# Moments and normalisations of three batches in tile pieces behind the maxima of the cross attention units

## What is computed

```
def _layernorm(x, axis=-1, eps=1e-05):
    m = jnp.mean(x, axis=axis, keepdims=True)
    v = jnp.var(x, axis=axis, keepdims=True)
    return (x - m) / jnp.sqrt(v + eps)

    x = x + _L0_attn_ref(_layernorm(x, axis=-1), ...)
    x = x + _L0_xattn_ref(_layernorm(x, axis=-1), ctx_1024, ctx_1024, ...)
    x = x + _L0_ffn_ref(_layernorm(x, axis=-1), ...)
```

## Time and profile before

| | us |
|---|---|
| median of 3 runs | 828.49 |
| lowest and highest | 826.69, 833.39 |
| the profiled execution | 834.13 |
| its span in the trace | 832.0 |

### The profile page before, as it was taken

How to read it: one execution, slowest core, us unless ns; L and a number is a source line. 1 busy time by engine, 2 the same in 40 slices (tenths; PEclk the granted TensorE clock), 3 DMA queues, 4 the chain that set the end, 5 groups by cost and what they waited for, 6 DMA issues and landing times.

```text
span 832.0 us, 14945 instructions
## 1 busy us (share of the span) xinstructions
PE 676.5 (81%) x4693; PEld 328.5 (39%) x4698; DVE 589.4 (71%) x1606; ACT 414.0 (50%) x708; POOL 282.6 (34%) x502
## 2 busy tenths in 40 slices
PE   2758998989888896079999952677999989998987
PEld 1324454435344444045666631222332323324443
DVE  3857788776556765657878745788889898953574
ACT  1332665655655542013333312156788777885454
POOL 4742454544523144703223220122323142331310
PEclk9875999989988858579999985569999999999898
DMA  7543654482233215211111123321223011000000
GB/s 218 159 175 119 208 181 142 137 274 72 70 99 87 74 42 156 77 33 40 44 41 40 45 68 126 101 77 52 65 90 127 27 52 51 3 2 1 2 25 26
DMA packets 74780, 71.27 MB, mean 86 GB/s; under 512 B 14560, under 2 KB 67168, under 8 KB 74704
## 3 DMA queue, kind: packets, MB, share of 16 engines
q1 hardware_dynamic: 72000, 64.84, 25.3%
q0 software_dynamic: 2272, 4.69, 1.8%
q10 hardware_dynamic: 432, 0.79, 0.3%
HBM read 41.90 MB, written 28.00 MB: 84 GB/s over the span
## 4 chain that ended last, share of the span: by engine, by line
PE 60%; DVE 19%; issue 7%; DMA 5%; POOL 4%; ACT 4%; SPq 1%; DVEq 0%; POOLq 0%; ACTq 0%
PE bank_pv L733 11%; DVE mx L591 11%; PE bank_turn L575 8%; PE bank_scores L2025 5%; PE bank_scores L685 4%; PE bank_scores L1775 4%; PE bank_turn L1760 4%; PE bank_scores L1760 4%; PE bank_turn L752 3%; POOL routed_tokens L1727 2%; PE bank_scores L1768 2%; PE bank_turn L528 2%; DVE stats L450 1%; DMA stk<-stack_A 1%; PE bank_turn L794 1%
## 5 line engine op out<-in xcount | busy, mean ns | idle before, releaser
L591 DVE TENSOR_REDUCE mx<-bank_turn 128x1 f32<-128x512 f32 (+3 forms) x452 | 260.4, 615 | 58.8 <-PE bank_turn L580 29.6
L575 PE MATMUL bank_turn<-stk 64*128 64x128 bf16 (+3 forms) x708 | 164.2, 322 | 31.2 <-DVE mx L591 20.4
L685 PE MATMUL bank_scores<-stk 64*128 64x512 bf16 (+4 forms) x576 | 176.3, 373 | 4.7 <-ACT probs L706 3.6
L710 ACT ACTIVATE probs<-bank_scores 128x1024 f32<-128x1024 f32 (+4 forms) x160 | 116.9, 769 | 101.6 <-PE bank_scores L685 100.3
L706 ACT ACTIVATE probs<-bank_scores 128x512 f32<-128x512 f32 x256 | 138.6, 605 | 35.5 <-PE bank_scores L685 34.5
L733 PE MATMUL bank_pv<-probs,vsl 128*32 128x512 f32 (+4 forms) x1152 | 142.9, 570 | 2.6 <-POOL probs L718 1.6
L575 PEld LDWEIGHTS bank_turn<-stk 64*128 64x128 bf16 x708 | 58.2, 101 | 133.4 <-DVE mx L591 63.9
L718 POOL TENSOR_SCALAR_AFFINE_SELECT probs<-probs 128x256 f32<-128x256 f32 x128 | 51.6, 408 | 72.3 <-ACT probs L710 70.7
L1743 POOL DMA_INDIRECT expert_outputs<-probs,y_at x39 | 37.3, 958 | 101.4 <-DVE probs L1662 98.8
L477 POOL TENSOR_TENSOR rstd<-var,mhalf 128x4 f32<-128x4 f32 x24 | 25.4, 1056 | 115.8 <-DVE var L456 115.7
L1807 ACT COPY okT<-bank_scores 128x512 f32<-128x512 f32 x39 | 22.9, 587 | 81.2 <-PE bank_scores L1768 81.2
(11 more groups left out here) (297 smaller groups left out, 1140.9 us busy)
## 6 DMA issues: line engine op xcount, KB each, us to landing
stk<-stack_A SPq DMA_DIRECT2D x64, 256.0 KB, 3.3
w<-in_M_w SPq DMA_DIRECT2D x12, 512.0 KB, 4.9
stack_A<-parts SPq DMA_DIRECT2D x15, 384.0 KB, 3.1
stack_A<-fill SPq DMA_DIRECT2D x8, 512.0 KB, 5.3
stk<-stack_X SPq DMA_DIRECT2D x16, 256.0 KB, 2.7
stack_A<-parts SPq DMA_DIRECT2D x15, 256.0 KB, 3.3
probs<-routed_tokens SPq DMA_DIRECT2D x39, 65.0 KB, 1.9
b_gated<-in_M_b SPq DMA_DIRECT2D x1, 2048.0 KB, 11.2
```

Of the source, the lines that this page charges most:

```text
L575: mm = e.matmul(o, stk[r, slot, 0, pp, qt * P:(qt + 1) * P], stk[r, slot, 1, pp, 0:keys], start=True, stop=not a.causal)
L591: e.tensor_reduce(o.rearrange("p h q -> p q h"), bank_of((g, m))[:, 0:k * wide].rearrange("p (q h k) -> p q h k", q=len(tiles), h=len(hs)) ...
L685: mm = e.matmul(score_bank(g, kt, i)[0:a.kp, 0:S - q0], stk[r, slot, 1, pp, kt * P:kt * P + a.kp], stk[r, slot, 0, pp, q0:S], start=True, ...
L710: e.activation(probs[0:a.kp, probs_of(g, kt), j:HG:2, 0:n], bank_scores[0:a.kp, 2 * j:2 * j + 2, 0:n], ACT.Exp, scale=1 / math.sqrt(HD)).t ...
```

## The change

A table APART_IN names three units and batches: 20 (X0, 3), 24 (M0, 0), 28 (M0, 1). In such a unit each of the four maxima on VectorE is followed by the `bn_stats` of one tile; the `bn_aggr` and the variance follow `neg`. In the unit after it (21, 25, 29) each of the four maxima is followed by the subtract and multiply of one tile. The blocks of moments in units 19, 23 and 27 and of normalisations in units 20, 24 and 28 are gone. The helpers are split by tile; where they are called for a whole batch they issue what they issued before. NORM_IN is unchanged, so Pool's norm_pool stays in units 20, 24 and 28; the orders of TensorE, ScalarE, Pool and SP are unchanged.

```
-MOMENTS_IN = {5: (X0, 0), 9: (X0, 1), 13: (X0, 2), 19: (X0, 3), 23: (M0, 0), 27: (M0, 1), 31: (M0, 2), 33: (A1, 3), 37: (X1, 0), 40: (F1, 0), 41: (X1, 1),
+MOMENTS_IN = {5: (X0, 0), 9: (X0, 1), 13: (X0, 2), 31: (M0, 2), 33: (A1, 3), 37: (X1, 0), 40: (F1, 0), 41: (X1, 1),
+APART_IN = {20: (X0, 3), 24: (M0, 0), 28: (M0, 1)}
...
         def moments_dve(e, ln, b):
+            for j in range(QT):
+                tile_stats_dve(e, ln, b, j)
+            variance_dve(e, ln, b)
+
+        def tile_stats_dve(e, ln, b, j):
             n = norm_number(ln, b)
+            if j == 0:
+...
+            e.bn_stats(stats[:, j, :], tile_of(4 * b + j)).then_inc(s_stat, 1)
+
+        def variance_dve(e, ln, b):
             e.wait_ge(s_stat, QT * (n + 1))
 ...
+        def normalise_tile(e, ln, b, j):
+            if j == 0:
+...
+            i = e.tensor_scalar(normal(ln, b)[:, j, :], tile_of(4 * b + j), mv[:, j, 0:1], rstd[:, j:j + 1],
+                                ALU.subtract, ALU.mult)
+            if j == QT - 1:
+                i.then_inc(s_xn, 1)
...
                 for i in range(4):
                     for k in beside[i]:
                         max_dve(e, *k)
+                    if g in APART_IN:
+                        after, b = APART_IN[g]
+                        tile_stats_dve(e, after.ln, b, i)
+                    if g - 1 in APART_IN:
+                        after, b = APART_IN[g - 1]
+                        normalise_tile(e, after.ln, b, i)
...
             if a is X0:
                 if g + 2 <= last_of_stream(g):
                     neg_of(e, g + 2)
+                if g in APART_IN:
+                    after, b = APART_IN[g]
+                    variance_dve(e, after.ln, b)
                 beside_dve(e, g - 1, "b")
                 beside_dve(e, g, "a")
-                if g in NORM_IN:
-                    after, b = NORM_IN[g]
-                    normalise(e, after.ln, b)
                 if g in MOMENTS_IN:
```

More of the change, by code:

```diff
@@ L440, in moments_dve @@
         def moments_dve(e, ln, b):
+            for j in range(QT):
+                tile_stats_dve(e, ln, b, j)
+            variance_dve(e, ln, b)
+        def tile_stats_dve(e, ln, b, j):
             n = norm_number(ln, b)
[L443 to L450, removed]
+            if j == 0:
+                if ln == 0:
+                    e.wait_ge(s_x0 if b == 0 else s_x, 16)
+                else:
+                    e.wait_ge(*x_at[(ln - 1, b)])
+                wait(e, s_xn, n)
+                take_wait(e)
+            e.bn_stats(stats[:, j, :], tile_of(4 * b + j)).then_inc(s_stat, 1)
+        def variance_dve(e, ln, b):
+            n = norm_number(ln, b)
             e.wait_ge(s_stat, QT * (n + 1))
@@ L462, in normalise @@
         def normalise(e, ln, b):
+            for j in range(QT):
+                normalise_tile(e, ln, b, j)
+        def normalise_tile(e, ln, b, j):
             n, ahead = norm_number(ln, b), norm_ahead(ln, b, 1)
[L465 to L473, removed]
+            if j == 0:
+                e.wait_ge(s_rstd, n + 1)
+                if ahead is not None:
+                    e.wait_ge(*turned_at[ahead])
+                if ln == M0.ln:
+                    e.wait_ge(s["values"], UN)
+            i = e.tensor_scalar(normal(ln, b)[:, j, :], tile_of(4 * b + j), mv[:, j, 0:1], rstd[:, j:j + 1],
+                                ALU.subtract, ALU.mult)
+            if j == QT - 1:
+                i.then_inc(s_xn, 1)
         def norm_pool(e, ln, b):
```

## The result

| | before | after |
|---|---|---|
| median of the runs compared, us | 829.12 (4 runs) | 837.93 (4 runs) |
| lowest and highest | 826.69, 833.39 | 835.62, 838.20 |
| the profiled execution | 834.13 | 838.20 |
| its span | 832.0 | 836.0 |

The ratio is 1.0095 (95% interval 1.0049 to 1.014): the changed kernel is slower by about 1%, and its time lies 1.9 us above the upper end of the predicted range. The interval leaves out 1, so a change of just under 1% could be told from none here, against what the prediction says.

A forecast was written before the change was run, and what follows sets the result against it. TensorE sets the pace (60% of the span), waiting for VectorE's otok in the cross units. Terms -0.8 + 1.6 + 1.9 + 0 - 1.2 = +1.5 us give 835.6, carried to the median 830.0; range 821 to 836.

The forecast's parts named there:

- the predicted range: Whole kernel's time, 8 in 10: 821 to 836 us.
- the lower end: VectorE: a maximum with its bn_stats 0.65 us in units 20, 24, 28; with its subtract-multiply 0.71 in 21, 25, 29.
- -0.8: Start of norm_pe in units 21, 25, 29: together -1.3 us at the cheapest piece costs, taken as -0.8.
- Rival 1: VectorE's alternating pieces don't overlap: pairs at 0.77 and 0.82 us, 2 us more, 832.0 us; chance 0.10.
- Rival 2: TensorE's clock stays at its upper level around the longer wait: -7.3 us, 821.2 us; chance 0.17.
- the same jobs at full clock: TensorE from norm_pe to the next unit: 0.66 + 1.07 + 0.66 + 0.2 + 1.1 = 3.5 us.
- rivals 2 and 3: TensorE's clock stays up: 821.2 us, chance 0.17; or also no new wait at norm_pe: 814.9 us, chance 0.05.
- rival 4: Low stretches of 19.3 us in pairs one and two also, over units 22, 23, 26, 27: +11, 841 us; chance 0.08.
- unit 30: Low stretch behind the third pair may end early, shortening unit 30 by 2.5 us, or linger; half taken, -1.2.
- the terms: Cross units: norm_pe -0.8, rest of the three pairs +1.6, +1.9 and 0, unit 30 -1.2; sum +1.5 us.
- carried to the median: Whole kernel: 835.6 us by the profiled execution's time, 0.7% above the median of 828.49, becomes 830.0.

The follow-up runs named there:

- the kernel with the wait filled: Changed kernel with seven matmuls of constants issued before the wait of norm_pe in units 21, 25 and 29: 824.88 us against 830.93, ratio 0.9941.
- the lengthened old ones: Kernel before with four more bn_stats behind the moments of units 19, 23 and 27, lengthening the waits for otok: 831.74 us against 829.22, ratio 1.0057.
- added work behind them: Changed kernel with seven constant matmuls ahead of the finish transposes of units 21, 25 and 29, behind the wait: 840.5 us against 829.22, ratio 1.016.
- the kernel with more filling: Changed kernel with seven constant matmuls in each new wait and four in each of two earlier waits (units 17, 18): 829.23 us against 827.71, ratio 1.002.
- the transposes later: Changed kernel with norm_pe behind the products, finish transposes and turn, and ScalarE's copy behind pv_out: 837.12 us against 830.93, ratio 1.009.

## Why the prediction failed

**Right: the waits for `otok` go.** No item of units 20, 24 and 28 waits over 0.3 us for it. Not foreseen were waits of 0.36 for `neg` and 0.39 for `otok` around the start of units 21, 25 and 29, 2.2 us over the three pairs.

**Right: they come back at norm_pe, longer.** "Some 2.1 us" were forecast; 1.99, 2.00 and 1.98 came. TensorE had its items done at 255.93 (forecast 256.0), and the transposes started at 257.92 in a unit 20 that began 0.10 us earlier than before (forecast 258.15 to 259.0).

**The pieces were cheaper than the lower end.** VectorE's timeline in units 20 and 21:

```profile
251.11 0.48 DVE L608 TENSOR_REDUCE mx<-bank_turn 128x4 f32<-128x308 f32 x1 [0.18 <-PE bank_turn L592]
251.51 0.29 DVE L457 BATCH_NORM_STATS2 stats<-x_sb 128x6 f32<-128x128 f32 x1
...
251.72 0.46 DVE L608 TENSOR_REDUCE mx<-bank_turn 128x4 f32<-128x308 f32 x1
252.10 0.28 DVE L457 BATCH_NORM_STATS2 stats<-x_sb 128x6 f32<-128x128 f32 x1
...
255.85 0.47 DVE L608 TENSOR_REDUCE mx<-bank_turn 128x4 f32<-128x308 f32 x1
256.24 0.34 DVE L487 TENSOR_SCALAR xn<-x_sb,mv,rstd 128x128 f32<-128x128 f32 x1
256.50 0.47 DVE L608 TENSOR_REDUCE mx<-bank_turn 128x4 f32<-128x308 f32 x1
```

A maximum and its `bn_stats` take 0.57 to 0.61 us (forecast 0.65 to 0.77), a maximum and its normalisation 0.65 (0.71 to 0.82): each starts some 0.08 us before the other ends, in both orders. From the start of its unit 20, 24 or 28 norm_pe comes after 7.31, 7.31 and 7.36 us, against 7.54, 7.75 and 8.57 before: -1.9 us where -0.8 was forecast. Rival 1, no overlap, is out. The Trainium skill's rule on which it leaned ("VectorE: DVE Perf Modes", "The DRAIN you can't avoid") doesn't hold for these pairs; the same section adds that an operation which isn't held starts earlier, and with that sentence the rows agree.

**Right: the lower clock follows.** From norm_pe to the next unit it was to take 6.0 us three times; it took 6.18, 5.09 and 5.98 (13.49 less 7.31 and so on). In the second pair the clock fell only near 281.5, 1.1 us after the wait, a little later than costed. Rival 2, a clock that stays up, is out for this kernel; it is what the fillings make of it. The terms of the same jobs at full clock add to 3.7, not to the 3.5 that the prediction writes; the kernel with the wait filled takes 3.39 there in unit 21 (258.32 to 261.71). Only rivals 2 and 3 use that sum.

**Wrong by 3.1: units 26 and 27.** The step "The low stretch lasts 6.2 us or more, so units 22 and 26 are mostly clear of it" holds for unit 22 (+0.16). Behind the second wait the stretch lasted 13.5 us and units 26 and 27 took 13.29. That is rival 4 in part: in one of its two places, and with 13.5 us where it has 19.3.

**Wrong by 1.2: unit 30.** The stretch behind the third wait was to let go of it half the time; it covers it to the end (0.50 over all of its 6.67 us). With the three pairs at +0.9 where the terms gave +2.7, these make 838.2 of the 835.6 forecast for the profiled execution.

**Wrong by 5.3: "carried to the median".** This is the step that failed most. The prediction took 5.6 us off its sum, from 835.6 to 830.0, because the profiled execution of before lay that far above the median. But what lay above the median was its low clock: 33.3 us at 1.2 GHz, when other executions of the same kernel had 26.9 or 9.9. The forecast itself said that the new waits bring the lower clock. An account built on a throttled execution, with a cause that keeps it throttled, has nothing to be carried down to: the changed kernel's profiled execution is 0.3 us above its own median. The terms came to +4.0 where +1.5 was forecast; of the 7.9 us between forecast and median they are 2.6, and the carrying is 5.3. The unevenness also stood in the rows: 6.2 us behind the wait of unit 20 and 19.3 behind that of unit 28, after waits of 1.30 and 1.58, ought to have raised the question how steady such stretches are from execution to execution.

**What stays open.** Why 2 us waits are followed by 13.5 us at 1.2 GHz in some places of the changed kernel, by 6.7 in the lengthened old ones and by 3.2 to 6.7 with added work behind them; whether the length of a wait, its place or something else makes the new waits cost more than the old; what decides how long a stretch follows the same wait (6.5 us or none behind the second, 6.6 to 20.3 behind the third); and why the kernel with more filling has two groups of runs.

**A faster version.** The changed kernel with its new waits filled (824.88, ratio 0.9941) is the fastest complete kernel here against the one before; the kernel before with its old waits filled (825.88, 0.9949) can't be told from it. The gain comes from the filling, not from the pieces.

## What to carry to other kernels

When work moves off one wait, find what its engine ends last and who waits for that: the pieces took away 4.2 us of waits and brought 8.2. Before a sum on one profiled execution is carried to the median, look at its granted clock beside that of other runs: what a throttled profile has above the median may be taken off the sum only if the change leaves the clock free to recover. And where a short wait of TensorE can't be removed, a few constant matmuls into the bank that is taken next are worth more here than the wait itself.

## What the runs showed of the hardware

- The same wait of TensorE in the same place of the same kernel was followed by very different times at 1.2 GHz from execution to execution: 6.5, 0 and 6.7 us behind the second wait (1.30 us), 20.3, 6.6 and 16.9 behind the third (1.58). All waits of 1.95 us and more that were looked at in units 20 to 29 (13, in five traces) were followed by at least 3.2 us of it; of the old waits of 1.29 to 1.59 us, 10 of 11 were (in four traces), so the wait's length alone parts little.
- Waits that are not removed but broken up by three matmuls into 0.68 and 0.71 us were not followed by it in the trace. That is no safe length: with the transposes later, waits of 0.84 and 0.67 us in unit 29 were followed by 6.7 us of it.
- A stretch at the lower level costs some 0.35 us for each us of it: from the end of the first wait to the first matmul of L1775 it is 8.3 us more in the one of two executions of the kernel before that has 23.4 us more of low clock.
- Two different VectorE operations in turn overlap as one repeated does: 0.57 to 0.61 us for a maximum of 0.46 to 0.48 and a `bn_stats` of 0.28.
